# Two-layer mixture-of-experts kernel, last stage: one register load instruction per engine for all dynamic tiles, and a place of its own in SBUF for every tile's rows

## The reference, cut to what matters

```
logits = x_flat @ gate_w.T
probs = softmax(logits)
topk_probs, topk_idx = top_k(probs, 2)
hidden = relu(einsum('th,ehf->tef', x_flat, w1) + b1)
all_out = einsum('tef,efh->teh', hidden, w2) + b2
gathered = take_along_axis(all_out, topk_idx[:, :, None], axis=1)
y_flat = sum(gathered * topk_probs[:, :, None], axis=1)
x = x + y_flat
```

## Time and profile before

| | us |
|---|---|
| median of 3 runs | 519.46 |
| lowest and highest of them | 518.76, 521.85 |
| the profiled execution, its device time | 516.84 |
| its span in the trace | 514.8 |
| last stage in the trace: from the end of the weight splits to the end | 374.9 to 514.8 |

### The profile page before, as it was taken

How to read it: one execution, slowest core, us unless ns; L and a number is a source line. 1 busy time by engine, 2 the same in 40 slices (tenths; PEclk the granted TensorE clock), 3 DMA queues, 4 the chain that set the end, 5 groups by cost and what they waited for, 6 DMA issues and landing times.

```text
span 514.8 us, 9104 instructions
## 1 busy us (share of the span) xinstructions
PE 437.1 (85%) x2391; PEld 367.1 (71%) x2391; DVE 403.0 (78%) x932; ACT 351.8 (68%) x766; POOL 205.0 (40%) x196
## 2 busy tenths in 40 slices
PE   8998999999999998999889899997019888888840
PEld 7984787777777776887767688886009787788830
DVE  2576699999999999998976999889817675667621
ACT  2335688889988888998888687985018675677710
POOL 3125343342244555230002206336600775676780
PEclk9996799999999999999989999999557998899985
DMA  3883344448544444453997112001350436676616
GB/s 101 224 217 117 140 164 163 163 173 282 218 163 169 173 187 180 188 225 123 355 361 218 46 55 84 18 28 40 110 159 1 54 72 150 130 177 173 124 18 228
DMA packets 49366, 76.85 MB, mean 149 GB/s; under 512 B 8949, under 2 KB 36278, under 8 KB 45494
## 3 DMA queue, kind: packets, MB, share of 16 engines
q1 hardware_dynamic: 36454, 59.84, 34.9%
q10 hardware_dynamic: 5232, 12.27, 6.4%
q0 software_dynamic: 7648, 4.36, 6.1%
HBM read 50.69 MB, written 18.77 MB: 135 GB/s over the span
## 4 chain that ended last, share of the span: by engine, by line
DVE 31%; PE 27%; issue 17%; DMA 14%; ACT 4%; POOL 3%; DVEq 3%; SPq 1%; ACTq 1%; POOLq 0%
DVE hid_lo L1068 10%; PE ps L1359 5%; PE ps L1360 5%; PE ps L1361 5%; DVE hid_lo L1157 4%; DVE yg L1062 4%; DMA out_d<-ysb,xrow 3%; DMA xrow<-disp 3%; DMA rawf<-in_L_ffn_w_dram 2%; DMA out_dram<-xtok 2%; PE ps L1637 2%; DVEq L1294 2%; POOL out_dram L742 2%; PE ps L1429 2%; DMA out_dram<-ysb,xrow 1%
## 5 line engine op out<-in xcount | busy, mean ns | idle before, releaser
L1068 DVE TENSOR_TENSOR hid_lo<-yg,hid_hi 128x512 fp32r<-128x512 f32 x124 | 97.2, 784 | 0.0
L797 ACT ACTIVATE hid<-ps,bias_cur 128x512 f32<-128x512 f32 x128 | 86.5, 676 | 11.4 <-PE ps L1361 10.6
L818 ACT ACTIVATE hid_hi<-yg 128x512 fp32r<-128x512 f32 x124 | 77.8, 628 | 20.5 <-DVE yg L1062 19.6
L630 POOL TENSOR_TENSOR w2l<-raw,w2h 128x128 fp32r<-128x128 f32 x32 | 25.3, 791 | 108.7 <-ACT w2h L767 108.7
L853 ACT ACTIVATE hid<-ps,cols 128x512 f32<-128x512 f32 (+3 forms) x84 | 52.8, 629 | 18.5 <-PE ps L1361 12.7
L1359 PE MATMUL ps<-in_hi,w1h 128*128 128x512 f32 x128 | 53.8, 420 | 6.3 <-POOL w1l L630 5.8
L742 POOL DMA_INDIRECT out_dram<-ysb,xrow x24 | 39.5, 1644 | 43.5 <-DVE ysb L1343 37.9
L1157 DVE TENSOR_TENSOR hid_lo<-hid,hid_hi 128x512 fp32r<-128x512 f32 (+3 forms) x84 | 50.5, 624 | 7.6 <-ACT hid_hi L857 6.5
L703 POOL DMA_INDIRECT disp<-stage,idx x32 | 34.0, 1062 | 50.3 <-issue 30.2
L1062 DVE TENSOR_TENSOR yg<-hid,h_f 128x512 f32<-128x512 f32 x60 | 50.6, 844 | 1.6 <-DMA h_f<-gt_d 1.0
L1361 PE MATMUL ps<-in_hi,w1l 128*128 128x512 f32 x128 | 51.3, 401 | 0.0
(11 more groups left out here) (232 smaller groups left out, 1209.0 us busy)
## 6 DMA issues: line engine op xcount, KB each, us to landing
gb<-gt_d SPq DMA_DIRECT2D x15, 1024.0 KB, 4.6
h_f<-gt_d SPq DMA_DIRECT2D x14, 1024.0 KB, 4.5
disp<-empty ACTq DMA_DIRECT2D x16, 616.5 KB, 6.8
w1d<-wf SPq DMA_DIRECT2D x15, 512.0 KB
rawf<-in_L_ffn_w_dram SPq DMA_DIRECT2D x16, 256.0 KB, 2.9
xrow<-disp SPq DMA_DIRECT2D x23, 137.0 KB, 2.5
raw<-in_L_ffn_We_dram SPq DMA_DIRECT2D x2, 960.0 KB, 8.4
nat<-in_x_dram SPq DMA_DIRECT2D x8, 128.0 KB, 3.1
```

The costliest lines, as they stand in the source:

```text
L797: nc.scalar.activation(hid0[:, m % 4, :], bank(4 + m % 4), ACT.Gelu, bias=bias0_cur[:, e_par:e_par + 1]).then_inc(s_hid0, 1)
L818: nc.scalar.activation(hid_hi0[:, m % 8, :], src[:, m % 4, :], ACT.Copy).then_inc(s_hi0, 1)
L1068: V.tensor_tensor(hid_lo0[:, m % 8, :], src[:, m % 4, :], hid_hi0[:, m % 8, :].bitcast(F32), ALU.subtract).then_inc(s_lo0, 1)
```

## The change

There are two edits. First, on SP, PE and DVE the numbers of `tab` are read by one load instruction of 15 registers (two on SP: first rows and experts), each followed by 15 pairs of the same register operation and check as before. Second, `xrow` has a place for each of the 23 tiles: 16 of them in `xrow_a`, on ground that the weights `wc2` of the step before held, and 7 in `xrow_b`, where the ring was. A load waits for no landing any more and each tile has its own semaphore. SP now loads the 8 static tiles, reads its registers, copies the weights of tiles 8 and 9, loads the 15 dynamic tiles in a row, and then copies the weights of tiles 10 to 22.

```diff
-XR = 7
+XR = 16
...
-        xrow = at("xrow", 8 * KB, [P, XR, 2, ROW], F32)
+        xrow_a = at("xrow_a", 96 * KB, [P, XR, 2, ROW], F32)
+        xrow_b = at("xrow_b", 8 * KB, [P, NTAU - XR, 2, ROW], F32)
...
-        s_ld = [sem(f"s_ld{k}") for k in range(XR)]
+        s_ld = [sem(f"s_ld{k}") for k in range(NTAU)]
...
+        def xrow(t):
+            return xrow_a[:, t, :, :] if t < XR else xrow_b[:, t - XR, :, :]
...
             def load(t):
 
-                dst = xrow[:, t % XR, :, :]
-                if t >= XR:
-                    added(sp, t - XR)
-                if t < STATIC:
-                    rows_of = disp_rs[0:TS, t, :]
-                else:
-                    first = sp.value_load(tab[0:1, 0, t - STATIC:t - STATIC + 1], min_val=0,
-                                          max_val=(RANKS - TS) * S1 + EF)
-                    rows_of = disp[bass.ds(first, TS, step=S1), :]
-                sp.dma_start(dst, rows_of.rearrange("(a p) c -> p a c", p=P)).then_inc(s_ld[t % XR], 16)
+                rows_of = disp_rs[0:TS, t, :] if t < STATIC else disp[bass.ds(first_of[t - STATIC], TS, step=S1), :]
+                sp.dma_start(xrow(t), rows_of.rearrange("(a p) c -> p a c", p=P)).then_inc(s_ld[t], 16)
 
             def weights(t):
 
                 j = t - STATIC
-                e = sp.value_load(tab[0:1, 1, j:j + 1], min_val=0, max_val=EF - 1)
+                e = expert_of[j]
...
             sp.wait_ge(s_disp, 16 * TILES * KF)
-            for t in range(XR):
+            for t in range(STATIC):
                 load(t)
             sp.wait_ge(s_tab, 2)
+            _, first_of = nc.values_load_multi_w_load_instructions(
+                tab[0:1, 0, 0:DYN], engines=[mybir.EngineType.SP], min_val=0, max_val=(RANKS - TS) * S1 + EF)
+            _, expert_of = nc.values_load_multi_w_load_instructions(
+                tab[0:1, 1, 0:DYN], engines=[mybir.EngineType.SP], min_val=0, max_val=EF - 1)
             weights(STATIC)
             weights(STATIC + 1)
-            for t in range(XR, NTAU):
+            for t in range(STATIC, NTAU):
                 load(t)
-                if STATIC + 2 <= t - 1:
-                    weights(t - 1)
-            weights(NTAU - 1)
+            for t in range(STATIC + 2, NTAU):
+                weights(t)
...
-            expert_of = [dve.value_load(tab[0:1, 1, j:j + 1], min_val=0, max_val=EF - 1) for j in range(DYN)]
+            _, expert_of = nc.values_load_multi_w_load_instructions(
+                tab[0:1, 1, 0:DYN], engines=[mybir.EngineType.DVE], min_val=0, max_val=EF - 1)
```

More of the change, by code:

```diff
@@ L743, in _ @@
                         out=(out_rows, out2)[t % 2],
-                        out_offset=bass.IndirectOffsetOnAxis(ap=xrow[:, t % XR, a, D:D + 1].bitcast(U32), axis=0),
+                        out_offset=bass.IndirectOffsetOnAxis(ap=xrow(t)[:, a, D:D + 1].bitcast(U32), axis=0),
                         in_=ysb[:, t % 3, a, :], in_offset=None, bounds_check=NT - 1, oob_is_err=False,
@@ L901, in exps @@
                     act.wait_ge(s_g, t - 3)
-                A.activation(exf[:, t % 4, :, :], xrow[:, t % XR, :, D + 1:ROW], ACT.Exp).then_inc(s_exf, 1)
+                A.activation(exf[:, t % 4, :, :], xrow(t)[:, :, D + 1:ROW], ACT.Exp).then_inc(s_exf, 1)
             for t in range(2):
@@ L1596, in turn @@
             def turn(t):
-                pe.wait_ge(s_ld[t % XR], 16 * (t // XR + 1))
+                pe.wait_ge(s_ld[t], 16)
                 if t >= 2:
@@ L1600, in turn @@
                 for a in range(2):
-                    op = M.transpose(bank(t % 2)[:, a * P:(a + 1) * P], xrow[:, t % XR, a, 0:D], ident[:])
+                    op = M.transpose(bank(t % 2)[:, a * P:(a + 1) * P], xrow(t)[:, a, 0:D], ident[:])
                 op.then_inc(s_tr, 1)
@@ L1644, in _ @@
             pe.wait_ge(s_tab, 2)
-            expert_of = [pe.value_load(tab[0:1, 1, j:j + 1], min_val=0, max_val=EF - 1) for j in range(DYN)]
+            _, expert_of = nc.values_load_multi_w_load_instructions(
+                tab[0:1, 1, 0:DYN], engines=[mybir.EngineType.PE], min_val=0, max_val=EF - 1)
             for t in range(2):
```

## The result

The changed kernel takes 503.61 us (median of 4 runs, 502.08 to 504.58) against 519.71 us before (4 runs): ratio 0.968, 95% interval 0.964 to 0.973, so 16.1 us faster. Timed once more beside other kernels it had a ratio of 0.974 (0.970 to 0.979). The forecast was 501.0 us with a range of 495.5 to 508.5, a gain of 18.4 us.

The account below looks back on a forecast made before the run. The bound was taken to be a loop through three tiles: addition, landing, load, transpose, `out_of`, addition. Registers (4.0 us) plus ring (14.4) gave 18.4 us off the median 519.46, so 501.0 us, range 495.5 to 508.5.

Parts of the forecast that it names:

- What bounded the kernel: Last stage: a loop through three tiles (addition, landing, load, transpose, `out_of`, addition), not an engine, sets 22 steps of 4.57 us.
- Registers on DVE: Ahead of DVE's first `split_x`: one bulk load replaces 15 single ones, start at 381.2 instead of 385.21, gain 4.0 us.
- Registers on SP: SP's bulk loads behind the eight static loads: first dynamic load between 388 and 397, needed near 403, so cost nothing.
- The ring: First addition of tile 0 to that of tile 22: without the wait 86.1 us instead of 100.5, gain 14.4.
- first term: Tiles 0 to 9: POOL's two additions set the pace, nine steps of 3.85 us, 34.7 us.
- ten steps of 4.0: Dynamic tiles from 10 on: weight copies waiting for tile `t - 2` set the pace, 4.0 us per tile, 40.0 us.
- The sum against the median: The 18.4 us gain, worked out against the profiled execution (516.84 us), was taken off the median 519.46 unchanged, giving 501.0.
- Engines alone: Rival, chance 0.16: only engines bind, copies land quicker and the bulk load costs 0.3 us; gain 24.2, so 495.3 us.
- The copy of 5.0 us: Rival, chance 0.14: a dynamic tile's weight copy takes 5.0 us, 4.51 us per step; gain 13.3, so 506.1 us.
- The landing of additions: Rival, chance 0.11: `t` waits for the landing of `t - 2`; at 6.4 us, 4.31 per step, so 509.7 us.
- A collision as priced: Slower rival, chance 0.03: weight copies collide with additions; above 7.7 us per copy the gain goes, at 9 us 526.0.

## Why the prediction was right, and what was off

**What bounded the kernel.** Right, and shown by putting the wait back: with `t - 7` most of the gain of this part is gone (96.9 us), with `t - 8` it is there (88.4).

**Registers on DVE.** Predicted 4.0 us within 1.9 to 6.2, measured 4.6. The term that was off is the bulk load: I took 2.4 us as the middle between 0.3 and 4.6, and it takes 1.80 to 1.83 on DVE. The 15 pairs cost 4.6 (380.92 to 385.54) where I had 4.2. A third slip of 0.3 us goes with them: the sum let the first operation start at 374.8, 0.6 us behind the load's start, although a load of 0.3 us was assumed; the bulk load's excess was then added to the 0.6. The transposes were indeed not late. The rule of the Trainium skill that I weighed there ("Runtime: NRT & Kernel Launch", section "Instruction fetch mechanics", 200 ns per register in bulk) would give 3.0 us, an estimate. The trace doesn't agree: it has (1.82 - 0.304) / 14 = 0.11 us for each register after the first, and the measurement decides. The rule is right in that a bulk load is not free of its registers.

**Registers on SP.** Right: its two loads took 1.59 and 1.38 us, no tile from 8 on waited for rows, and the run with single loads on SP had nearly the same loop (87.6 us).

**The ring.** The sum was 34.7 for nine steps, 40.0 for ten and 11.4 for three. The changed trace has 34.7 (398.92 to 433.63), 40.3 (to 473.92) and 11.5 (to 485.40), so 86.5 against 86.1. That the terms fit so closely is in part luck. The size of the first term's step was wrong: it is 3.73 us and not 3.85. In these steps POOL runs without a wait for DVE (1.55 to 1.58 us and 0.30 twice), and PE, by the run with half the additions, allows no less either. Steps of 4.03, 3.90, 4.21 and 3.93 among them made the sum come out. The 1.62 us per addition that I took as POOL's own price contained long ones of up to 2.1 us, and these go once the copies are early. The ten steps of 4.0 came from the copies, since with a third place they fall to 3.7, but not in the way that was said. The prediction had every copy hold up its tile, 7.97 us for two tiles. In the changed trace PE's steps are mostly 3.73, and five late copies of 15 cost it 3.9 us. Of these POOL, which had work in hand, waited for 1.1 us more than its usual 0.30:

```profile
446.07 2.04 POOL L742 DMA_INDIRECT out_dram<-ysb,xrow_a  x1 [1.40 <-DVE ysb L1344]
...
460.17 2.09 POOL L742 DMA_INDIRECT out_d<-ysb,xrow_a  x1 [0.30 <-issue]
```

The larger share are the additions of these ten tiles, 33.1 us in all against 31.0 with three places. The prediction priced no such lengthening: the 3.0 us by which these ten steps exceed 3.73 each are two effects of about 1 and 2 us, where it had one.

**The sum against the median.** This is where I look for the 2.3 of the 18.4 us that are missing; it is argued from two profiles. The step was "I take off the same amount there": I carried the gain from one profiled execution over to the median. The stretch ahead of the stage differs by 5 us between two profiles of the kernel before and its loop by 1.6, 98.9 us in the second profile. With that pair of profiles the two parts come to 4.6 + 11.9 = 16.5, near the 16.1 measured. The 100.5 was one draw.

**The rivals.** Engines alone (495.3) fell, since PE still waits for copies. The copy of 5.0 us came true for single ones: PE started 5.13 us after one copy's start (434.76 to 439.89, with 1.37 us of waiting), but the mean step stayed at 4.0. The landing of additions did not show. A collision as priced, copies of over 7.7 us, did not show either, though additions and copies do seem to lengthen each other by a few us over the stretch.

## What to carry to other kernels

A ring whose place is freed by the far end of the pipeline makes a loop over (places minus the tiles in between). Divide the loop's length by that number and compare it with the busiest engine's time per tile: here 13.2 / 3 = 4.4 bound and 13.2 / 4 = 3.3 didn't, so one place more was worth nearly as much as sixteen, and the next ring (two places for the weights) was where the next gain lay. Before a gain from a profiled execution is set against a median, look at how far two profiles of the same kernel differ ahead of the place that is edited.

## What the runs showed of the hardware that I had not expected

- A load of 15 registers from one row of `tab` takes 1.80 to 1.83 us on DVE, 1.77 to 1.87 on PE and 1.37 to 1.61 on SP, one of a single register 0.27 to 0.31 at the median and up to 1.0. The register operation and the check behind each number cost 0.31 us on DVE (15 operations start from 381.0 to 385.3), nearly three times the 0.11 us of a further register.
- POOL's indirect DMAs of the same size have a median of 1.55 us and at most 1.83 with a third place for the weights. In the changed kernel they take up to 2.09 us. Why the timing of SP's copies changes them was not tried.
- The kernel before had medians of 520.7 us on one chip and of 515.6 and 513.3 us on another, the two ends over 1% apart. The write of `tab`, ahead of which nothing had changed, came between 365.6 and 377.4 us in the thirteen profiles.
